# Moving row statistics from VectorE to ScalarE, region offsets to TensorE, and splitting one wait on expert weights

## The reference

```python
# attention branch: gated memory with a decay, per batch row of 256 steps
gate = sigmoid(x @ Wg + bg);  store = (x @ Wv) * gate * scale
mem = associative_scan(decay 0.95)(store);  que = sigmoid(x @ Wq + bq)
x = x + (mem * que * scale) @ Wo                      # x = layernorm(x) inside
# cross branch: p = layernorm(x), kv = ctx @ W_k.T + b_k
out = p @ kv;  sim = (out @ kv.T) * 256 ** -0.5
mu = mean(sim);  var = var(sim)
x = x + softmax((sim - mu) * rsqrt(var + 1e-6) * ln_gamma + ln_beta)
# mixture: n = layernorm(x) as 1024 rows
logits = n @ router_w;  e = argmax(logits);  xs = n * sigmoid(max(logits))
out[rows of e] = (silu(xs @ gate_w[e]) * (xs @ up_w[e])) @ down_w[e]
x = x + out + (silu(n @ sh_gate) * (n @ sh_up)) @ sh_down
```

## Time and profile before

| | us |
|---|---|
| median of 3 runs (138.19, 138.51, 139.47) | 138.51 |
| the profiled execution | 139.09 |
| its span, first to last instruction | 137.2 |
| PE busy | 116.0 (85%) |
| DVE busy | 82.8 (60%) |
| ACT busy | 75.1 (55%) |
| POOL busy | 75.3 (55%) |

### The profile page before, as it was taken

How to read it: one execution, slowest core, us unless ns; L and a number is a source line. 1 busy time by engine, 2 the same in 40 slices (tenths; PEclk the granted TensorE clock), 3 DMA queues, 4 the chain that set the end, 5 groups by cost and what they waited for, 6 DMA issues and landing times. The chain is left out here.

```text
span 137.2 us, 2564 instructions
## 1 busy us (share of the span) xinstructions
PE 116.0 (85%) x663; PEld 94.3 (69%) x663; DVE 82.8 (60%) x290; ACT 75.1 (55%) x193; POOL 75.3 (55%) x118
## 2 busy tenths in 40 slices
PE   0099999999999888988997997499999999999600
PEld 0059889869779574857887865378888888888300
DVE  2673099928979998739785872556454546454000
ACT  3335787695666859149573362144556465655500
POOL 5207070573856793891838799300665466456680
PEclk9999999999999999879999999999999999999975
DMA  4997992065252552104102291963426451351200
GB/s 126 249 264 207 358 302 76 0 202 185 76 160 76 193 190 76 70 16 153 62 22 81 98 313 40 301 213 81 78 56 118 72 88 42 36 63 20 30 1 0
DMA packets 18924, 16.44 MB, mean 120 GB/s; under 512 B 4320, under 2 KB 18656, under 8 KB 18912
## 3 DMA queue, kind: packets, MB, share of 16 engines
q1 hardware_dynamic: 15792, 13.56, 32.1%
q0 software_dynamic: 2544, 2.17, 9.6%
q10 hardware_dynamic: 576, 0.56, 1.2%
HBM read 11.82 MB, written 5.38 MB: 125 GB/s over the span
## 5 line engine op out<-in xcount | busy, mean ns | idle before, releaser
L480 POOL DMA_INDIRECT out_dram<-tq,tid x15 | 23.3, 1556 | 23.4 <-ACT tq L670 12.3
L466 POOL TENSOR_TENSOR gu_lo<-stage,gu_hi 128x512 fp32r<-128x512 f32 x16 | 20.3, 1286 | 2.1 <-ACT gu_hi L527 2.0
L461 POOL DMA_INDIRECT x_sorted<-xs,dest x8 | 8.6, 1074 | 5.3 <-DVE dest L821 3.1
L527 ACT CAST gu_hi<-stage 128x512 fp32r<-128x512 f32 x16 | 9.4, 618 | 0.0
L1136 PE MATMUL bV<-dn,xT 128*128 x32 | 8.3, 383 | 0.8 <-ACT xT L664 0.8
L1086 PE MATMUL bV<-shd,xn 128*128 128x256 f32 x32 | 7.9, 389 | 0.8 <-ACT xn L628 0.7
L928 PE MATMUL bT<-ident,xn 128*128 128x128 f32 x16 | 2.9, 311 | 6.6 <-DVE xn L716 6.6
L658 ACT ACTIVATE tg<-bG,meta 128x256 f32<-128x256 f32 x8 | 3.8, 474 | 7.8 <-PE bG L922 7.8
L884 DVE SCALAR_TENSOR_TENSOR tg<-tg,bG 128x256 f32<-128x256 f32 x8 | 3.4, 422 | 7.6 <-ACT tg L658 7.6
L1003 PE MATMUL bO<-wo,tq 128*128 128x256 f32 x32 | 7.9, 389 | 0.0
L703 DVE BATCH_NORM_STATS2 bn<-res 128x6 f32<-128x256 f32 x16 | 6.0, 415 | 2.5 <-DMA res<-in_x_dram 2.4
(11 more groups left out here) (204 smaller groups left out, 359.5 us busy)
## 6 DMA issues: line engine op xcount, KB each, us to landing
stage<-in_L_ffn_gate_w_dram SPq DMA_DIRECT2D x8, 256.0 KB, 3.4
stage<-in_L_ffn_up_w_dram SPq DMA_DIRECT2D x8, 256.0 KB, 3.1
dn<-in_L_ffn_down_w_dram SPq DMA_DIRECT2D x8, 256.0 KB, 3.4
xs<-x_sorted SPq DMA_DIRECT2D x15, 136.0 KB, 2.2
res<-in_x_dram SPq DMA_DIRECT2D x4, 256.0 KB, 3.8
out_dram<-res SPq DMA_DIRECT2D x4, 256.0 KB, 3.2
x_sorted<-pad SPq DMA_DIRECT2D x5, 136.0 KB, 1.8
x_sorted<-pad ACTq DMA_DIRECT2D x4, 136.0 KB, 2.5
```

The costliest lines, as they stand in the source:

```text
L461: g.indirect_dma_start(x_sorted, bass.IndirectOffsetOnAxis(dest[:, t:t + 1], 0), xs[:, t, :], None, bounds_check=E * REGION - 1, oob_is_er ...
L466: g.tensor_tensor(units[n][2], stage[:, n % RING], f32(units[n][1]), ALU.subtract).then_inc(unit_lo, 1)
L480: g.indirect_dma_start(out_rows, bass.IndirectOffsetOnAxis(tid[:, s:s + 1], 0), ry[:, s % TILE_RING, :], None, bounds_check=N - 1, oob_is_ ...
L527: a.copy(units[n][1], stage[:, n % RING]).then_inc(unit_hi, 1)
```

## The change

Four things change together.

1. **Statistics.** The variance of x after the attention branch and of the similarities are sums of squares on ACT (`squares2`, `sim_squares`) in place of `bn_stats` on DVE. The mean of x comes from a sum that `residual2` now makes while it adds. For this MEM_SCALE is folded into the value weights (unit 2). The step `sim_stats` is gone.
2. **Region offsets.** The start of each expert's region is put into PSUM by one more matmul in `rank`, from a row `region`, in place of an addition in `destination`; a conversion there is gone too.
3. **Waits.** `gate_up` of tiles 0 to 3 waits for its own expert's splits only, by four numbers of the table (`units_ahead`) that PE reads into registers one by one; tile 4 waits for all. The wait before `rows_turn:0` is gone.
4. **Order.** All four step lists are written anew.

```diff
@@ -32,46 +32,46 @@
...
-    shared_down:0 rank:2 turn3:3 shared_gu:2 router:3 shared_turn:1 rank:3 shared_down:1
-    shared_turn:2 shared_gu:3 shared_down:2 shared_turn:3 shared_down:3
+    shared_turn:1 router:2 shared_gu:2 turn3:3 rank:2 shared_down:1 router:3 shared_turn:2 rank:3
+    shared_gu:3 shared_down:2 shared_turn:3 shared_down:3
...
@@ -404,16 +412,17 @@
...
             def sim_eps(b):
-                pool.wait_ge(stats[LN2], b + 1)
-                g.tensor_scalar(eps_row[:, b, :], mv[:, LN2, b, :, 1], SIM_EPS / SIM_SCALE ** 2, LN_EPS * SIM_EPS / SIM_SCALE ** 2,
+                pool.wait_ge(sm["squared2"], (b + 1) * TB)
+                g.tensor_scalar(eps_row[:, b, :], ssq2[:, b, :], SIM_EPS / SIM_SCALE ** 2 / D, (LN_EPS - 1.0 / D ** 2) * SIM_EPS / SIM_SCALE ** 2,
...
             def rsqrt(kind, b):
-                pool.wait_ge(stats[kind], b + 1)
...
+                    pool.wait_ge(sm["sim_squared"], (b + 1) * TB)
...
-                    g.tensor_tensor(vareps[:, kind, b, :], mv[:, kind, b, :, 1], eps_row[:, b, :], ALU.add).then_inc(eps_added[kind], 1)
+                    g.tensor_tensor(vareps[:, kind, b, :], sim_ssq[:, b, :], eps_row[:, b, :], ALU.add).then_inc(eps_added[kind], 1)
...
+                    pool.wait_ge(stats[kind], b + 1)
...
@@ -426,13 +435,11 @@
...
             def centre(b):
-                pool.wait_ge(stats[LN2], b + 1)
+                pool.wait_ge(sm["x2_made"], (b + 1) * TB)
...
-                g.tensor_scalar(minus_m[:, b, :], mv[:, LN2, b, :, 0], -1.0, -1.0 / S, ALU.mult, ALU.add).then_inc(sm["minus_made"], 1)
-                for i in range(TB):
-                    last = g.tensor_scalar(xs[:, b * TB + i, D + 3:D + 4], mv[:, LN2, b, i, 0:1], 1.0 / S, None, ALU.add)
-                last.then_inc(sm["mean_made"], 1)
+                g.tensor_scalar(minus_m[:, b, :], x2_sum[:, b, :], -1.0 / D, -1.0 / D, ALU.mult, ALU.add).then_inc(sm["minus_made"], 1)
+                g.tensor_scalar(xs[:, b * TB:(b + 1) * TB, D + 3], x2_sum[:, b, :], 1.0 / D, 1.0 / D, ALU.mult, ALU.add).then_inc(sm["mean_made"], 1)
...
@@ -515,6 +522,23 @@
...
+            def squares2(b):
+                act.wait_ge(sm["minus_made"], b + 1)
+                act.wait_ge(sm["x2_made"], (b + 1) * TB)
+                for i in range(TB):
+                    if b * TB + i >= 1:
+                        act.wait_ge(sm["squared2"], b * TB + i)
+                    a.activation(unused2[:, :], res[:, b * TB + i, :], ACT.Square, bias=minus_m[:, b, i:i + 1],
+                                 accum_out=ssq2[:, b, i:i + 1]).then_inc(sm["squared2"], 1)
+            def sim_squares(b):
+                act.wait_ge(sm["sim_done"], b + 1)
+                for i in range(TB):
+                    if b * TB + i >= 1:
+                        act.wait_ge(sm["sim_squared"], b * TB + i)
+                    a.activation(unused_s[:, :], psS[:, i, :], ACT.Square, scale=1.0 / 16.0,
+                                 accum_out=sim_ssq[:, b, i:i + 1]).then_inc(sm["sim_squared"], 1)
...
@@ -524,7 +548,10 @@
...
             def weight_hi(n):
...
-                a.copy(units[n][1], stage[:, n % RING]).then_inc(unit_hi, 1)
+                if n == PROJ - 1:
+                    a.mul(units[n][1], stage[:, n % RING], MEM_SCALE).then_inc(unit_hi, 1)
+                else:
+                    a.copy(units[n][1], stage[:, n % RING]).then_inc(unit_hi, 1)
...
@@ -719,7 +746,10 @@
...
             def weight_lo(n):
...
-                v.tensor_tensor(units[n][2], stage[:, n % RING], f32(units[n][1]), ALU.subtract).then_inc(proj_lo, 1)
+                if n == PROJ - 1:
+                    v.scalar_tensor_tensor(units[n][2], stage[:, n % RING], MEM_SCALE, f32(units[n][1]), ALU.mult, ALU.subtract).then_inc(proj_lo, 1)
+                else:
+                    v.tensor_tensor(units[n][2], stage[:, n % RING], f32(units[n][1]), ALU.subtract).then_inc(proj_lo, 1)
...
@@ -748,12 +778,8 @@
...
-                    v.scalar_tensor_tensor(res[:, t, :], psO[:, i, :], MEM_SCALE, res[:, t, :], ALU.mult, ALU.add).then_inc(sm["x2_made"], 1)
-                statistics(LN2, b, lambda i: res[:, b * TB + i, :], "x2_made")
-            def sim_stats(b):
-                dve.wait_ge(sm["sim_done"], b + 1)
-                statistics(SIM, b, lambda i: psS[:, i, :])
+                    v.tensor_tensor_reduce(res[:, t, :], psO[:, i, :], res[:, t, :], 1.0, 0.0, ALU.add, ALU.add,
+                                           x2_sum[:, b, i:i + 1]).then_inc(sm["x2_made"], 1)
...
@@ -812,13 +838,10 @@
...
-                v.tensor_tensor(ps_rank, ps_rank, io_reg[:, :, :], ALU.add).then_inc(sm["row_made"], 1)
-                dve.wait_ge(sm["row_made"], n)
...
-                v.tensor_reduce(dest_f[:, tiles], row_e[:, :, :], AX.X, ALU.add).then_inc(sm["dest_summed"], 1)
-                dve.wait_ge(sm["dest_summed"], n)
-                v.tensor_copy(dest[:, tiles], dest_f[:, tiles]).then_inc(sm["dest_made"], 1)
+                with nc.allow_low_precision(reason="one row number and zeros are added, whole and below 2 ** 24"):
+                    v.tensor_reduce(dest[:, tiles], row_e[:, :, :], AX.X, ALU.add).then_inc(sm["dest_made"], 1)
...
@@ -843,6 +866,7 @@
...
+                v.tensor_scalar(units_ahead[:, :], te_f[:, 0:EARLY], E - 1.0, float(UNITS), ALU.min, ALU.mult)
...
@@ -863,13 +887,15 @@
...
             def split_router():
+                dve.wait_ge(consts_made, 1)
+                v.tensor_copy(region[:, :], io_reg[0:1, :, :].rearrange("p t e -> p (t e)")).then_inc(rw_split, 1)
...
-                dve.wait_ge(rw_split, 1)
+                dve.wait_ge(rw_split, 2)
@@ -1040,7 +1066,9 @@
...
-                T.matmul(ps_rank, below[:, :], onehot[:, first:first + TB, :], start=True, stop=False)
+                pe.wait_ge(rw_split, 3)
+                T.matmul(ps_rank, ones[0:1, :], region[:, :], start=True, stop=False)
+                T.matmul(ps_rank, below[:, :], onehot[:, first:first + TB, :], start=False, stop=False)
...
@@ -1114,6 +1142,10 @@
...
             def gate_up(s, r, e, reused):
+                if s < EARLY:
+                    pe.wait_ge(unit_lo, ahead[s] + (SHARED_LO + UNITS))
+                elif s == EARLY:
+                    pe.wait_ge(unit_lo, len(units) - PROJ)
...
@@ -1137,8 +1169,8 @@
...
+            ahead = [pe.value_load(units_ahead[0:1, s:s + 1], min_val=0, max_val=UNITS * (E - 1)) for s in range(EARLY)]
...
-            pe.wait_ge(unit_lo, len(units) - PROJ)
...
```

More of the change, by code:

```diff
@@ L41 @@
-    shared_turn:2 shared_gu:3 shared_down:2 shared_turn:3 shared_down:3
+    turn1:0 turn_ctx:0 turn_ctx:1 turn_wk:0 gate:0 value:0 query:0 kv:0 turn1:1 kv:1 recall:0 gate:1
+    value:1 turn1:2 query:1 turn2:0 turn_kv:0 gate:2 turn1:3 context_mix:0 recall:1 similarity:0
+    value:2 query:2 turn2:1 gate:3 context_mix:1 recall:2 similarity:1 query:3 turn2:2 turn3:0
+    value:3 context_mix:2 router:0 shared_gu:0 recall:3 similarity:2 rank:0 turn3:1 turn2:3
+    shared_turn:0 context_mix:3 router:1 similarity:3 shared_gu:1 turn3:2 shared_down:0 rank:1
@@ L55 @@
-    weight_hi:19 weight_hi:20 shared_turned:3
+    weight_hi:0 weight_hi:1 weight_hi:2 turned1_hi:0 turned_wk:0 turned_ctx:0 gate_tanh:0 norm1:1
+    turned_ctx:1 query_tanh:0 kv_bias:0 turned1_hi:1 norm1:2 weight_hi:3 kv_bias:1 weight_hi:4
+    weight_hi:5 weight_hi:6 gate_tanh:1 turned1_hi:2 norm1:3 query_tanh:1 turned_kv:0 turned2:0
+    weight_hi:7 weight_hi:8 squares2:0 mixed:0 turned1_hi:3 centred:0 gate_tanh:2 weight_hi:9
+    weight_hi:10 sim_squares:0 weight_hi:11 query_tanh:2 turned2:1 squares2:1 gate_tanh:3 centred:1
@@ new lines @@
+    mixed:1 softmax_exp:0 sim_squares:1 weight_hi:12 turned2:2 turned3_hi:0 squares:0 query_tanh:3
+    mixed:2 weight_hi:13 squares2:2 weight_hi:14 softmax_exp:1 score_tanh:0 centred:2 shared_tanh:0
+    squares:1 sim_squares:2 turned3_hi:1 turned2:3 weight_hi:15 squares2:3 mixed:3 softmax_exp:2
+    shared_turned:0 sim_squares:3 score_tanh:1 shared_tanh:1 turned3_hi:2 squares:2 centred:3
+    weight_hi:16 softmax_exp:3 shared_turned:1 weight_hi:17 score_tanh:2 weight_hi:18 turned3_hi:3
+    shared_tanh:2 squares:3 shared_turned:2 weight_hi:19 score_tanh:3 shared_tanh:3 weight_hi:20
@@ L56 @@
+    shared_turned:3
 """.split()
 DVE_ORDER = """
[L59 to L63, removed]
@@ L64 @@
-    turned3_lo:2 residual3:3 route:2 shared_hidden:1 destination:2 turned3_lo:3 shared_add:0 route:3
-    shared_hidden:2 destination:3 slot_table:3 shared_add:1 shared_hidden:3 shared_add:2
-    shared_add:3
+    stats1:0 norm1:0 weight_lo:0 weight_lo:1 turned1_lo:0 weight_lo:2 stats1:1 stats1:2 memory:0
+    turned1_lo:1 centre_kv:0 residual2:0 stats1:3 centre_kv:1 turned1_lo:2 memory:1 residual2:1
+    turned1_lo:3 memory:2 sim_scale:0 residual2:2 residual3:0 turned3_lo:0 sim_scale:1 memory:3
@@ L67 @@
+    route:0 residual3:1 residual2:3 shared_hidden:0 turned3_lo:1 sim_scale:2 destination:0 route:1
```

(5 more changed lines are left out.)

36 lines of the change are left out of this document (17 added, 19 removed).

## The result

The changed kernel takes **142.76 us** (median of 4 runs, 142.03 to 143.29); the kernel before, run beside it, 138.43. The ratio is 1.029, interval 1.024 to 1.034: slower by 4.3 us, and outside the predicted range. The profiled execution is the one of 142.03, its span 140.3.

The account below looks back on a forecast made before the run. PE was taken as the bound, with the start of its tile stage deciding: 1.45 earlier, less 0.75 for a clock fall, gives -0.7 on the median of 138.51, so 137.8 us; 8-in-10 range 135.6 to 139.7.

Parts of the forecast that it names:

- the five register loads: Ahead of `rows_turn:0` in PE's queue, four `units_ahead` values and the table: 0.5 each, 2.5 in all, ending at 85.4.
- The start: First `rows_turn:0`, beginning of the tile stage: forecast 85.4 in place of 86.85, 1.45 earlier.
- `rank:3` was to end at 74.6: Dense stage: 75.1 before, plus 2.4 for work moved ahead, less 1.3 of waits and 1.6 of clock.
- the 1.6 of the clock in the dense stage: Time lost at half clock in `shared_gu:0`, forecast to come back in the new order; bounds 0 and 1.6.
- the rival of a second fall: Dense stage keeps its fall to half clock, costing 1.6: 139.4 in all; chance 0.18.
- From there to PE's end: From `rank:3` to the end of PE's dense stage: 10.7 before, 2.2 moved ahead, 8.5 forecast.
- From `rank:3` to the rows: Chain from `rank:3` to rows in SBUF: 11.3 before, 10.3 forecast, 0.6 from the moved split and 0.4 from `destination`.
- The move of statistics: Eight pairs at 0.95, 7.6 us from DVE to ACT; gives or costs only through waits.
- The early tiles: `gate_up` waiting only for its own expert's splits: worth nothing, as the splits end at 84.1, before 85.4.
- The fall behind the gap: Clock falls in PE's idle time ahead of `rows_turn:0`, to half rate until 88.6: 0.75 lost in the tile stage.
- Loads at 0.1 each: Rival at `rows_turn:0`: pipelined register loads and a kept clock, gains 1.95 to 2.95, 136.6 to 135.6; chance 0.29.
- ACT as the bound: Rival in the dense stage: added squares in ACT's queue delay PE in two batches, 1.9 more, 139.7; chance 0.13.

Follow-up runs that it names:

- e14: The changed kernel with two early numbers read in place of four (tiles 0 and 1 wait for their own expert): 137.88 us, ratio 0.984.
- e3: The changed kernel with the four early numbers read twice, nine register reads in all: 144.97 us, ratio 1.044.
- e1: The changed kernel with its third part (waits) undone: one wait for all splits, one read of the expert table: 136.42 us, ratio 0.981.
- e5: e1 with the statistics back on DVE, no squares on ACT: 138.62 to 143.12 us, no ratio; the profiled execution took 138.69.
- e11: e1 with its table read cut in two, tile 0 and the other fourteen, without checks: 141.19 us (138.40 to 142.78), no ratio.
- e2: The changed kernel with the four early numbers fetched by one read, their four checks kept: 138.65 us, ratio 0.999.
- e13: e1 with the table read in two pieces without checks, fourteen experts and then the last: 136.37 us, ratio 0.977.
- e12: The changed kernel with the expert table (te) read ahead of the four early numbers: 141.44 us, ratio 1.008.
- e10: e1 with its one table read cut into five, without checks: 137.63 us, ratio 0.979.
- b2: The kernel before with the third part (waits) of the change alone: 143.48 us, ratio 1.034.
- e7: e1 with the router's matmuls made 256 columns wide by filler: 137.52 us, ratio 0.988.
- e8: e7 with the filler columns written by POOL in place of DVE: 139.35 us, ratio 1.005.
- e9: e8 with 17 filler matmuls of 256 columns added in PE's waits behind `rank:3`: 140.87 us.

## Why the prediction was wrong

**The failed step is the five register loads "in PE's queue ahead of `rows_turn:0`", and their price.** I put them behind PE's end, 82.9 (my own terms, 74.6 + 8.5, give 83.1), with 2.5 in all, and said that their cost had no row on PE. Three things were off.

- Their price. 0.5 was enough for a read of one value (0.30 to 0.50 in the changed kernel). But `te` is fifteen values in one read, 1.76, and this stood in the trace of before. The bounds checks that each early number brings (the rows "ISA x2" in the order that I quoted) I did not price: 0.3 each. And the `te` read took 2.75 in this kernel.
- Their place. They start with `shared_down:3`, and not behind it. The errors have opposite signs: 5.8 in place of 2.5, but 2.0 of it beside the matmuls. The gap was 3.95.
- Their cover. In the kernel before the one read ended 0.15 ahead of the matmuls, so these 1.97 were used up already, and only the wait of 1.06 for POOL's splits stood behind them. In the new order the rows are there as the matmuls end (84.69 and 84.63), so all that was added showed.

The rule of the Trainium skill that I weighed (DMA: Bandwidth & Descriptors, Latency and other measured facts), a floor of about 600 ns for a `tensor_load`, does not agree with these rows: reads of one value took 0.30 to 0.50 in the changed kernel. By it I would have said 85.9, nearer but for a wrong reason, since the rule prices neither the fifteen values nor the checks.

**The other terms.** The start was to be 85.4 and was 88.57.

- `rank:3` was to end at 74.6 and ended at 75.3: the 1.6 of the clock in the dense stage did not come back (the rival of a second fall, 0.18), and PE waited for 0.9 and not 1.8. The two errors cancel in part. Whether the clock stays up there differs between kernels with the same dense stage: where it did, `rank:3` ended at 73.8 (e14) and 74.1 (e3).
- From there to PE's end 8.5 were forecast and 9.3 measured, since another fall lies on `shared_gu:3` (4.41). No case held two falls in the dense stage.
- From `rank:3` to the rows 10.3 were forecast, 9.4 measured: there at 84.69, forecast 84.9. The scatter's start-up did take part of what the moved split gave (0.86 idle ahead of it). That the rows came on time is luck in part: `rank:3` was 0.7 late and the way behind it 0.9 short.
- The move of statistics: 7.6 us from DVE to ACT forecast, 7.3 measured on each (DVE 82.8 to 75.5, ACT 75.1 to 82.4).
- The early tiles gain nothing: right, by e1. The fall behind the gap: right as a kind, 0.75 forecast, 1.34 measured.

So the start is 3.2 and the clock 0.6 beyond the forecast, 3.8 in the span (140.3 against 137.2 - 0.7).

**The rivals.** Loads at 0.1 each (0.29) is refuted by the durations. ACT as the bound (0.13), my slower side, did not happen: no wait of PE before `rank:3` names an ACT copy, and e5 says that in this order the squares on ACT are the change's gain. No case of mine was slower by the reads, for I let them cost at most 0.7 each: five from 82.9 would end at 86.4, still ahead of the 86.85 before.

**What stays open**: why a `te` read took 1.6 to 1.86 in most kernels, 2.75 in the changed one and 4.98 (fourteen values) in e11. The DMA share does not tell it: 0.88 in the changed kernel's read, and 0.88 in e2's too, which took 1.6. About 1.0 of the gap of 3.95 is this longer read. Open too is what puts the clock's falls where they are, and why the changed kernel lies above 142 in all four executions, when others that share its dense stage differ in their falls.

## What to carry to other kernels

Here PE's register reads ran on its sequencer beside the last busy matmuls. Price such reads from their own rows, by the number of values and with their checks, and compare the sum with the work that covers it. Up to that cover, or up to the arrival of what the next step needs anyway, they are free (e13, e14); beyond it each 0.1 us shows. A finer wait must pay for its reads; here none was worth anything, and the best versions, e1 and e13, read once or twice and wait once. Try a change of four parts in parts: here one gave some 2 us, one took 6. And look at several profiles before you reason from a fall of the clock: the same dense stage had none, one or two.

## What was not expected of the hardware

A read of one value took 0.30 to 0.50 us, in e3 and e12 up to 0.60, of four 0.53, of eleven 1.32, of fifteen mostly 1.76: some 0.1 for each further value, an estimate from these. A bounds check took 0.3, an estimate from e10 and the changed kernel. In every kernel with a gap of 1.7 us or more ahead of the tile stage the clock was at half in that stage (in b2 and e3 from within the gap on), for 3.4 or 6.8 us, and the stage was 1.3 to 2.6 longer (44.41 in the changed kernel, 45.63 in e12). Below that it went either way: at half behind gaps of 0.9 to 1.1 in e7, e8 and e9, not behind 1.1 in the kernel before and 1.2 in e10.
